# Start-up of a one-core attention and mixture-of-experts kernel: who issues the one-off loads, when TensorE starts, and the list that fills the pipeline

## The reference

```python
x = x + layernorm(attention(layernorm(x)))      # 16 heads of 8, rope, causal softmax
x = x + layernorm(ffn(layernorm(x)))
# attention: q, k, v = h @ Wq + bq, h @ Wk + bk, h @ Wv + bv;  q, k = rope(q), rope(k)
#            softmax(mask(q k^T / sqrt(8))) v, then @ Wp + bp
# ffn: scores = softmax(h @ gate_w + gate_b); the 2 best of 16 experts, weights cw
#      y = sum_e cw_e (silu(h @ w1_e + b1_e) * (h @ w3_e + b3_e)) @ w2_e + cw @ b2
#      z = (silu(h @ sw1 + sb1) * (h @ sw3 + sb3)) @ sw2 + sb2     (shared expert)
#      result y + z
```

## Time and profile before

| | us |
|---|---|
| median of 3 runs | 1215.54 (1213.74 to 1216.63) |
| the profiled execution | 1213.77 |
| its span | 1211.3 |
| its mean granted TensorE clock | 0.941 of full |

### The profile page before, as it was taken

How to read it: one execution, slowest core, us unless ns; L and a number is a source line. 1 busy time by engine, 2 the same in 40 slices (tenths; PEclk the granted TensorE clock), 3 DMA queues, 4 the chain that set the end, 5 groups by cost and what they waited for, 6 DMA issues and landing times.

```text
span 1211.3 us, 26878 instructions
## 1 busy us (share of the span) xinstructions
PE 1068.8 (88%) x8520; PEld 701.6 (58%) x8520; DVE 847.2 (70%) x2283; ACT 713.9 (59%) x1569; POOL 837.4 (69%) x984
## 2 busy tenths in 40 slices
PE   2389999999999999999999999999857999999800
PEld 1245565666656566565666656655435888888600
DVE  4378788787787877878778777775232666666586
ACT  0107677676676766767667676677512555555434
POOL 4535669788787887878778777566663666666667
PEclk9559999999999999999999999999978999999955
DMA  4333333313323133231332313323122444544276
GB/s 92 97 106 101 86 97 92 111 55 123 110 82 112 55 122 105 88 110 57 118 106 92 100 57 119 96 69 119 56 64 79 124 125 124 158 125 123 93 232 184
DMA packets 104681, 126.16 MB, mean 104 GB/s; under 512 B 17422, under 2 KB 85344, under 8 KB 99936
## 3 DMA queue, kind: packets, MB, share of 16 engines
q1 hardware_dynamic: 91638, 104.54, 29.0%
q0 software_dynamic: 8704, 18.11, 4.2%
q10 hardware_dynamic: 4202, 1.81, 0.5%
HBM read 78.06 MB, written 45.42 MB: 102 GB/s over the span
## 4 chain that ended last, share of the span: by engine, by line
PE 83%; DVE 6%; POOL 2%; issue 2%; ACT 1%; DMA 1%; SPq 0%; POOLq 0%; DVEq 0%; ACTq 0%
PE heads_ps L1474 13%; PE score L1464 12%; PE wide L1502 11%; PE wide L1624 7%; PE wide L1439 7%; PE wide L1504 5%; PE score L1452 3%; PE wide L1605 3%; PE wide L1606 3%; PE score L1596 3%; PE misc L1482 2%; PE wide L1535 2%; PE wide L1622 2%; DVE mx L1276 2%; DVE f_st L1081 1%
## 5 line engine op out<-in xcount | busy, mean ns | idle before, releaser
L1276 DVE TENSOR_REDUCE mx<-wide 128x2 f32<-128x1024 f32 (+3 forms) x384 | 390.8, 1042 | 104.6 <-PE wide L1504 103.0
L946 ACT ACTIVATE values<-score 128x512 f32<-128x512 f32 (+1 forms) x704 | 375.0, 557 | 128.5 <-PE score L1464 100.2
L833 POOL TENSOR_SCALAR_AFFINE_SELECT values<-values 128x512 f32<-128x512 f32 x256 | 162.0, 639 | 140.9 <-ACT values L946 138.5
L1502 PE MATMUL wide<-qk 72*128 72x512 bf16 (+3 forms) x1024 | 246.9, 307 | 4.4 <-DVE mx L1276 3.2
L1464 PE MATMUL score<-qk 75*128 75x512 bf16 (+3 forms) x1024 | 239.9, 301 | 2.4 <-ACT values L946 1.9
L878 POOL DMA_INDIRECT token_scratch<-spread,e_id x144 | 137.3, 954 | 95.8 <-issue 75.1
L1504 PE MATMUL wide<-maskneg,identb 128*128 128x128 bf16 x1024 | 200.1, 224 | 0.0
L1474 PE MATMUL heads_ps<-values 128*32 128x512 f32 (+3 forms) x2048 | 171.0, 440 | 0.0
L822 POOL DMA_INDIRECT sorted_scratch<-zr,places x128 | 128.7, 1006 | 43.0 <-issue 22.2
L1464 PEld LDWEIGHTS score<-qk 75*128 75x128 bf16 x1024 | 89.2, 99 | 98.4 <-ACT values L946 44.9
L1502 PEld LDWEIGHTS wide<-qk 72*128 72x128 bf16 x1024 | 101.8, 99 | 60.0 <-issue 13.0
(11 more groups left out here) (196 smaller groups left out, 1978.2 us busy)
## 6 DMA issues: line engine op xcount, KB each, us to landing
qk<-parts_scratch SPq DMA_DIRECT2D x192, 192.0 KB
parts_scratch<-spread SPq DMA_DIRECT2D x16, 768.0 KB
qk<-sorted_scratch SPq DMA_DIRECT2D x144, 66.0 KB
front<-token_scratch SPq DMA_DIRECT2D x16, 512.0 KB, 4.0
xt<-attn_x SPq DMA_DIRECT2D x16, 256.0 KB, 6.0
xr<-attn_x SPq DMA_DIRECT2D x16, 256.0 KB, 6.9
x_scratch<-z SPq DMA_DIRECT2D x16, 256.0 KB, 6.5
shared_scratch<-s_out SPq DMA_DIRECT2D x16, 256.0 KB, 6.2
```

Source lines behind the costliest of these rows:

```text
L833: nc.gpsimd.affine_select(out=prob[n][:, :, 0:P], in_=prob[n][:, :, 0:P], compare_op=ALU.is_ge, fill=0.0, base=0, pattern=[[0, HG], [1, P] ...
L946: nc.scalar.activation(free_ap(prob[kb][:, hs_[0], :], [[1, N * len(hs_)]]), score[SCORE_RING.buffer(b, step)][:, 0:N * len(hs_)], ACT.Exp ...
L1276: nc.vector.tensor_reduce(mx[:, h0:h0 + len(hs_), j:j + 1], src, axis=AX.X, op=ALU.max).then_inc(p1_max, 1)
L1502: nc.tensor.matmul(o, q4[e][0:ROWS, h, j * P:(j + 1) * P], k4[e][0:ROWS, h, 0:L], start=True, stop=False)
```

## The change

1. The 14 loads of biases and shared-expert weights and the 1056 KB write of `blank` are issued by SP, right behind its attention weights, and no longer by ACT.
2. The nine copies behind `splits` are issued by SP in its body for i = -3, between the load of x of sequence 1 and the write of `spread` of sequence 0.
3. PE issues 12 matrix products of ones (128x512, bf16) into `heads_ps` before its first step. Nothing reads them. The function that does so, `kept_busy`, was used before the expert stage already and is only moved.
4. `START` is a new order of the same 87 steps. `ORDER`, `DRAIN` and the offsets are as they were.

```diff
+FIRST_FILL = 12
 START = (
-    "rstd@1 stats@1 normal@1 sin0@1 X@1 sin1@1 sin2@1 sin3@1 R@1 Q@1 rstd@2 normal@2 V stats@2 third0@1 third1@1 "
+    "X@1 rstd@1 normal@1 sin0@1 sin1@1 stats@1 sin2@1 sin3@1 R@1 rstd@2 normal@2 third0@1 Q@1 cos@1 third1@1 "
...
@@ SP, behind its attention weights
+            sp.dma_start(bias_f[0:E, 0:INTER], b1).then_inc(bias_in, 16)
...
+                sp.dma_start(sb3_col[0:m, c:c + 1], sb3[at:at + m].rearrange("(h o) -> h o", o=1)).then_inc(f_fw, 16)
+            sp.wait_ge(ident_ready, N_IDENT)
+            sp.dma_start(sorted_d[E * CAP:, :].rearrange("(n p) c -> p n c", p=P),
+                          free_ap(blank[:], [[1, SPARE], [1, ROW]], SPARE)).then_inc(spare_filled, 16)
@@ SP, body(i), behind the load of xt
+                if i == -3:
+                    sp.wait_ge(bias_split, 1)
+                    sp.wait_ge(rows_cleared, 5)
+                    for r in range(NPART):
+                        sp.dma_start(bias_rows[r * E:(r + 1) * E, :], bias_parts[0:E, r, 0:2 * INTER]).then_inc(bias_kept, 16)
+                        sp.dma_start(sb2_rows[r:r + 1, :], bias_parts[E:E + 1, r, 2 * INTER:]).then_inc(bias_kept, 16)
+                        sp.dma_start(sb1_rows[r:r + 1, :], bias_parts[E:E + 1, r, 0:2 * INTER]).then_inc(bias_kept, 16)
@@ ACT
-            act.dma_start(bias_f[0:E, 0:INTER], b1).then_inc(bias_in, 16)
...
-                    if step.what == "splits":
-                        act.wait_ge(bias_split, 1)
...
-                    elif step.what == "s":
+                    if step.what == "s":
@@ PE, before its body
+            kept_busy(FIRST_FILL)
```

More of the change, by code:

```diff
@@ L589, in _ @@
             sp.dma_start(sin_sb[:], sin).then_inc(weights_in, 16)
+            sp.dma_start(bias_f[0:E, 0:INTER], b1).then_inc(bias_in, 16)
+            sp.dma_start(bias_f[0:E, INTER:2 * INTER], b3).then_inc(bias_in, 16)
+            sp.dma_start(bias_f[0:E, 2 * INTER:], b2).then_inc(bias_in, 16)
+            sp.dma_start(bias_f[E:E + 1, 0:2 * INTER], row(sb1)).then_inc(bias_in, 16)
+            sp.dma_start(bias_f[E:E + 1, 2 * INTER:], row(sb2)).then_inc(bias_in, 16)
+            for w, s in ((sw1_sb[:], sw1), (sw3_sb[:], sw3),
+                         (sw2_sb[:, 0:NCH - 1, :], sw2[0:(NCH - 1) * P, :].rearrange("(c h) d -> h c d", h=P)),
+                         (sw2_sb[0:CH[-1][1], NCH - 1, :], sw2[CH[-1][0]:, :]),
+                         (gw_sb[:], gate_w), (gb_bc[:], row(gate_b).to_broadcast([P, E]))):
+                sp.dma_start(w, s).then_inc(f_fw, 16)
+            for c, (at, m) in enumerate(CH):
+                sp.dma_start(sb3_col[0:m, c:c + 1], sb3[at:at + m].rearrange("(h o) -> h o", o=1)).then_inc(f_fw, 16)
+            sp.wait_ge(ident_ready, N_IDENT)
+            sp.dma_start(sorted_d[E * CAP:, :].rearrange("(n p) c -> p n c", p=P),
+                          free_ap(blank[:], [[1, SPARE], [1, ROW]], SPARE)).then_inc(spare_filled, 16)
             def maxima_in(b, e, half):
@@ L1383, in _, with kept_busy @@
             pe.wait_ge(filled, 4)
+            def kept_busy(count):
+                for _ in range(count):
+                    nc.tensor.matmul(heads_ps[:], onesb[:], free_ap(onesb[:], [[0, NT], [1, P]]), start=True, stop=True)
+            kept_busy(FIRST_FILL)
             def body(i):
@@ L1575, in experts_of @@
                 return list(values)
-            def kept_busy(count):
-                for _ in range(count):
-                    nc.tensor.matmul(heads_ps[:], onesb[:], free_ap(onesb[:], [[0, NT], [1, P]]), start=True, stop=True)
             def x_across(n, k, r, j):
```

## The result

| | before | after |
|---|---|---|
| median of the comparison (4 runs each) | 1214.64 us | 1203.63 us |
| lowest to highest | 1213.36 to 1216.63 | 1202.59 to 1205.13 |
| profiled execution, its span | 1213.77, 1211.3 us | 1205.13, 1202.7 us |
| first scores start at | 88.14 us | 79.45 us |

The ratio after to before is 0.9907, with an interval of 0.9896 to 0.9919: 11.0 us faster by the medians, 8.6 by the spans of the two profiled executions. The time lies in the range given, 1202.5 to 1212.5.

What follows compares the result with a forecast made beforehand. PE bounds the kernel (busy 1068.8 of 1211.3 us); only the fill changes. First scores move from 88.14 to 81.0, 7.1 us, plus 0.4 for the clock: 1215.54 - 7.5 = 1208.0; 8-in-10 range 1202.5 to 1212.5.

Steps and rivals of the forecast that it cites:

- One for one: Behind the first scores PE is full, so what the first scores gain the end should gain too.
- likeliest case: The forecast as worked out, 1208.0 us with its own range 1205 to 1211; chance 0.72.
- Part 1: Start of the fill: with loads off ACT, Q of sequence 0 starts at 13.95 instead of 19.25, 5.3 us earlier.
- stall: SP's issues stalling as ACT's first did (4.37 us), named as a sign that the forecast is wrong.
- Part 2: 12 products before X and Q of sequence 0: cost 0 to 0.3 us, raised clock saves 1.1.
- Part 3: T of sequence 0 in the fill: done on DVE at 30.0 instead of 40.0, ten microseconds earlier.
- Part 4: SP's queue after `splits` and nine copies: write of `spread` leaves at 38.3 instead of 43.45, bounds 36.0 to 41.0.
- Part 5: p0 no longer waits for Q of sequence 2: starts at 51.5, 10.9 us earlier.
- Part 6: p chain grows by 3.8 to 29.5 us, now holding X and Q of sequence 2; first scores at 81.0.
- The clock did not stay up: Rival: PE's clock rises early and stays through the p chain, 12 us gained at first scores, 1203.5; chance 0.16.
- SP did not swallow the gain: Rival: SP's issues stall or the nine copies take longer, `spread` written at 41 or later, 1214.3; chance 0.08.
- x of sequence 3: Rival: this load lands near 75, DVE waits, first scores at 91, 3 us slower, 1218.5; chance 0.04.

Runs made afterwards that it cites:

- third run of after: The changed kernel run once more with no edit, beside new runs of the kernel before: 1205.22 us, ratio 0.9925.
- both runs with the copies late: Changed kernel with the nine copies on SP behind the 12 shuffles of sequence 0: 1245.07 us (ratio 0.9922, slower chip) and 1202.46 us (0.9897).
- sixth run: Changed kernel with the nine copies on SP moved behind the 12 shuffles of sequence 0, on the slower chip: 1245.07 us, ratio 0.9922.

## Why the prediction was right, and where its sizes were off

**One for one.** Right. The scores gained 8.7 us and the span 8.6. From the Q of iteration 1 to the end of the span it took 1081.0 to 1081.9 us in all ten profiles from chips of this speed, whatever the fill. The forecast of the time, 1208.0, was 4.4 above the first median and 2.8 above the two later ones. Of the 4.4, 0.9 is the median of before, which a fourth run brought down from 1215.54 to 1214.64; 1.2 is the gain, 7.5 for 8.7; and 2.3 is by how much the first medians differed beyond the 8.7, which the later ones did not repeat. So 1203.63 was just outside the likeliest case's own range, 1205 to 1211; 1205.16 and 1205.22 lie at its low end. What was short is the sum, by 1.6 us at the first scores (81.0 for 79.45, ahead of the 0.4 added for the clock around Q), and this is made of the following.

**Part 1.** Right to 0.4 us: Q at 13.59, for 13.95. The "stall" did move along in part, to `sin_sb` (2.38), b1 and b3 (0.95 and 1.09), and SP's issues ended at 17.94, inside the 15.1 to 18.9. The prediction had named such a stall as a sign that the forecast is wrong; it cost little in the new list, for nothing on the chain stood behind it but `sin_sb`, which Q waited for in seven of the ten profiles with products, by some 0.1 to 0.3 us. Costing x of sequence 1 at nothing held for this list only: it landed at 22.3, within 1.7 us of where its cover was said to end, and in the old list the same write ahead of it cost 3.85.

**Part 2.** The mechanism was right and the term too small in that execution: 1.78 for Q and 0.28 for X, 2.1 and not 1.1. Over ten profiles with these products Q took 1.96 to 2.00 in seven and 3.45 to 3.64 in three, so the mean gain of Q is 1.3. What was not foreseen is how it is missed: in none of the three did the clock rise too late. It rose during the products (they took 4.48 to 4.80 us, and X 0.66) and stood at 0.50 again from 13.4 to 14.1 us, just as Q, which starts at 13.4 to 13.7, began. In the profile of after it rose at 12.4 and fell at 19.2. Both halves of what the Trainium skill says (TensorE: Matmul & The Clock Gate, "What's actually happening"), that activity releases the throttle and that the moment varies from run to run, are now in the traces.

**Part 3.** DVE's T ended at 27.76, for 30.0; 2.1 of these 2.2 us are the clock of Q and X, for which the prediction took 1.1 off only at the end of part 4.

**Part 4.** The term that was mis-sized is `splits`: taken at 3.5, with 2.3 as the low bound, measured at 2.18. The bound failed because it was T's price, 1.23 us for 1024 elements, carried over to all four: the two casts took 0.39 for 480 elements and the two subtractions 0.65. Beside a busy POOL the same steps had spread over 5.1 us. The first cast is 0.92 there and 0.39 here. The trace of before has such a pair within `fold`: a cast of 128x128 to `bp_part` took 1.02 us at 33.39 beside a busy POOL and 0.23 at 35.73 beside an idle one. The Trainium skill (SBUF — State Buffer, "SBUF: two separate sides") says that GpSimd and some kinds of DVE instruction share one pair of ports, which one of them holds for a whole instruction. The traces agree so far, as POOL was idle from 27.63 to 30.52; no run here put POOL beside `splits` on purpose. With the 5.68 of the copies, for 5.75, the write left at 35.69, for 38.3, and below the 36.0 given as the bound. That SP's queue and not the data sets it was right, and the two runs without the copies ahead of it showed it.

**Part 5.** Here an error went the other way. From the write to p0 it took 15.1 us, for 13.2: the half of the shuffles landed 11.1 us behind the first issue, for 9.3. The 137 GB/s of the earlier trace rows were all the traffic of that stretch, and I gave it all to the first six shuffles. In the kernel after 143 GB/s flowed from 39.72 to 50.82, 1.6 MB, while these six are 1.18: a part of the second six, issued from 44.06 on, moved before the first six had all landed. In the other profiles of the new list the way from the write to p0 took 14.2 to 15.2 us but for one, the third run of after, with 16.6.

**Part 6.** Right: 28.63 us for 29.5, DVE waiting 2.51 for Q, for 2.6, and the clock at 0.56.

So the error of 1.6 us at the scores is made of three: 2.6 too late at the write, 1.9 too early from there to p0, and 0.9 too long in the p chain. Two errors of opposite sign made the sum better than its terms.

**The rivals.** The clock did not stay up, by the profile after and by the run with 12 more products, and where it did for ten microseconds (third run of after) the chain was only 0.8 us shorter. That the first median fell on that rival's 1203.5 is chance. SP did not swallow the gain, though it took 2.9 us of it. x of sequence 3 was issued at 50.76 and was there when DVE asked for it at 61.79, ten microseconds before the 72 from which it would have decided.

**What was not forecast** is that the loop can take some of a gain back, 1.5 to 2.0 us, when the clock rises 5.0 to 6.6 us behind the first scores rather than within 1.6. It did so in five of the fourteen profiles: the new list without products, the old list with loads on SP, with and without products, and both runs with the copies late. What decides it is open: it happened with the products and without them, and in either list.

## What to carry to other kernels

A fill is a chain of waits: before pricing an edit in it, write down for each engine and queue what it holds behind the step that moves, for an earlier step is worth only what the next wait lets through (5.2 and 4.8 us alone, 8.7 together; the products worth nothing under one list). Look at what a load waits behind on its own queue: with the loads on SP, one large write put behind the load of x was worth 3.85 us and a whole new order of steps no more than that. And take the price of an operation from a row of the same element type with the same neighbours at work, and never give a stretch's whole bandwidth to one of its transfers.

## What the runs showed of the hardware

- The same 12 products, 5.3 us at the start, were followed by a Q at 2.4 GHz in seven profiles and by one at 1.2 GHz in three, while the column of the granted clock showed 1.00 from the start of the span in either case. The slowest of these products took 0.63 us and the fastest 0.38, so part of that stretch was at the lower level: before the first change that the trace records the column says nothing.
- A clock that has risen can be gone again for the next work: in the sixth run it was up from 10.7 to 14.1 us, with PE busy in 1.22 of the 2.90 us from 10.70, and Q began at 13.68.
- A raised clock fell back inside the p chain: 1.00 in 50 to 52 us with PE busy in 1.18 of 2, 0.50 in 54 to 56 with PE busy in all of it. In the kernel after it was up from 67.0 to 70.4, in the third run of after from 67.1 to 77.3, in the same steps.
- The write of `spread` of sequence 1, issued at 50.27 behind the shuffles of sequence 0, was read back only at 60.41, 10.1 us later; the one of sequence 0, with nothing ahead, took 4.0. The Trainium skill (DMA: Bandwidth & Descriptors, "Queues, rings and completion order") says that work of one issuing engine is taken in ring order on each DMA engine; the trace agrees, though these two numbers do not tell that order from a mere sharing of the DMA engines.
- Issue of a DMA stalls now and then, whichever engine issues: 4.37 us on ACT before, 2.38, 1.62, 1.09 and 0.95 on SP after, beside a usual 0.4 to 0.6. All but the 1.62 lie between 5.9 and 10.9 us, behind the first 12 or 13 issues of SP and ACT together. The cause is open.
- ACT's table load, which before stood directly ahead of the first copy (17.22), ran at 6.41 with 5.16 us of idle time behind it: it does not wait for the data of the instruction that needs it.
- One chip of the same kind took 1256.38 us where the others took 1214. From the Q of iteration 1 to the end it took 1120.7 to 1126.7 us there, for 1081.0 to 1081.9; most of the difference lies behind about 850 us. What is slower there was not looked into.
